# Grouped attention: the two halves of the last three heads' partitions change places by transfers within SBUF, one sine product in place of two

## The reference, cut to what matters

```python
q = _layernorm(q, q_norm_w, q_norm_b)
k = _layernorm(k, k_norm_w, k_norm_b)
...
def _rope(x, cos, sin):
    xr, xi = (x[..., 0::2], x[..., 1::2])
    c, s = (cos[None, None], sin[None, None])
    out = jnp.stack([xr * c - xi * s, xr * s + xi * c], axis=-1)
    return out.reshape(x.shape)
q = _rope(q, cos, sin)
k = _rope(k, cos, sin)
k = jnp.repeat(k, rep, axis=1)
v = jnp.repeat(v, rep, axis=1)
scores = jnp.einsum('bhqd,bhkd->bhqk', q, k) / math.sqrt(D)
scores = jnp.where(causal[None, None], scores, -jnp.inf)
attn = jax.nn.softmax(scores, axis=-1)
out = jnp.einsum('bhqk,bhkd->bhqd', attn, v)
out = out.transpose(0, 2, 1, 3).reshape(B, S, H * D)
out = out * jax.nn.sigmoid(gate)
return out @ w_o.T
```

## Time and profile before

| | us |
|---|---|
| median of 3 runs | 1878.19 (1874.29 to 1879.25) |
| the profiled execution | 1874.4 |
| its span, first to last instruction | 1873.1 |
| PE busy | 1588.7 (85%) |
| DVE busy | 1240.9 (66%) |
| ACT busy | 910.1 (49%) |
| POOL busy | 334.2 (18%) |

### The profile page before, as it was taken

How to read it: one execution, slowest core, us unless ns; L and a number is a source line. 1 busy time by engine, 2 the same in 40 slices (tenths; PEclk the granted TensorE clock), 3 DMA queues, 4 the chain that set the end, 5 groups by cost and what they waited for, 6 DMA issues and landing times. The chain is left out here.

```text
span 1873.1 us, 16334 instructions
## 1 busy us (share of the span) xinstructions
PE 1588.7 (85%) x5242; PEld 861.0 (46%) x5242; DVE 1240.9 (66%) x2009; ACT 910.1 (49%) x1615; POOL 334.2 (18%) x208
## 2 busy tenths in 40 slices
PE   5998788788899999977989989767778777799998
PEld 2564354367544434433444444323323332347776
DVE  7685574433356446567786877569679899856665
ACT  5454344443322212268787878534565543325443
POOL 1001231231001101100000000000038666313332
PEclk8998899886789999988999989776789999999999
DMA  2003762350030000011010000200200000011110
GB/s 76 1 1 99 274 223 99 75 101 1 6 131 0 0 15 0 12 61 40 1 47 1 17 18 1 78 18 1 74 0 1 0 1 1 18 39 48 56 49 23
DMA packets 40729, 79.81 MB, mean 43 GB/s; under 512 B 9058, under 2 KB 26420, under 8 KB 38342
## 3 DMA queue, kind: packets, MB, share of 16 engines
q1 hardware_dynamic: 35558, 53.08, 9.4%
q0 software_dynamic: 5088, 25.69, 3.9%
HBM read 70.49 MB, written 7.22 MB: 41 GB/s over the span
## 5 line engine op out<-in xcount | busy, mean ns | idle before, releaser
L2872 POOL TENSOR_TENSOR s_bu<-s_rep,s_du 128x1024 f32<-128x1024 f32 x64 | 150.6, 2354 | 682.4 <-ACT s_rep L2789 599.3
L2726 DVE TENSOR_TENSOR_SCAN s_bu<-bank,s_bu 128x1024 f32<-128x1024 f32 x64 | 146.0, 2282 | 13.6 <-ACT bank L2798 13.5
L2961 PE MATMUL bank<-s_bu,ident 128*128 128x512 f32 x256 | 132.3, 642 | 0.9 <-DVE s_dl L2673 0.2
L159 PE MATMUL bank<-e_xs,e_wsp 128*128 128x512 f32 x528 | 127.7, 391 | 0.7 <-issue 0.7
L2798 ACT ACTIVATE bank<-s_dl,s_an 128x510 f32<-128x510 f32 x128 | 82.8, 682 | 75.4 <-DVE s_bu L2726 75.3
L159 PEld LDWEIGHTS bank<-e_xs,e_wsp 128*128 128x128 f32 x528 | 99.1, 188 | 22.7 <-issue 1.9
L159 PE MATMUL bank<-r_am,r_b 128*128 128x512 f32 x240 | 106.0, 593 | 1.4 <-DVE r_am L1712 1.4
L159 PE MATMUL bank<-conditioned,g_wqk 128*128 128x512 f32 x160 | 84.2, 654 | 0.3 <-POOLq L147 0.3
L1770 ACT ACTIVATE r_sl<-bank 128x512 f32<-128x512 f32 x28 | 16.7, 597 | 136.4 <-PE bank L159 133.2
L3067 DVE TENSOR_TENSOR e_s<-e_s,bank 128x512 f32<-128x512 f32 (+1 forms) x50 | 34.3, 687 | 69.3 <-ACT e_s L3199 69.3
L2742 DVE TENSOR_TENSOR s_bu<-s_bu,bank 128x1024 f32<-128x1024 f32 x64 | 76.6, 1197 | 5.1 <-PE bank L2892 4.9
(11 more groups left out here) (500 smaller groups left out, 3662.4 us busy)
## 6 DMA issues: line engine op xcount, KB each, us to landing
e_wgu<-in_e_gu SPq DMA_DIRECT2D x22, 256.0 KB, 2.6
b_vw<-b_values SPq DMA_DIRECT2D x48, 64.0 KB, 3.5
e_wd<-in_e_down SPq DMA_DIRECT2D x22, 128.0 KB, 2.6
r_w<-in_r_w SPq DMA_DIRECT2D x3, 896.0 KB, 8.4
g_wqk<-in_g_qk SPq DMA_DIRECT2D x4, 640.0 KB, 6.1
g_wgv<-in_g_gv SPq DMA_DIRECT2D x4, 640.0 KB, 3.9
g_wo<-in_g_wo SPq DMA_DIRECT2D x4, 512.0 KB, 3.5
m_sorted<-m_zero SPq DMA_DIRECT2D x1, 1920.0 KB, 13.2
```

What stands on the lines that cost most here:

```text
L159: last = e.matmul(out, lhs, rhs, start=start and n == 0, stop=stop and n == len(pairs) - 1, skip_group_check=True)
L2726: e.tensor_tensor_scan(b, flat(k.pairs[n % 2][:, :, :]), b, 0.0, ALU.mult, ALU.add).then_inc(k["s_scanned"].up(), 1)
L2872: e.tensor_tensor(m.bu[n % m.NBU][:, :, :], m.rep[:, 2 * np:2 * np + 2, :], m.du[:, et, half(h)].unsqueeze(1).to_broadcast([P, 2, HALF]), ...
L2961: summed = e.matmul(banks[6][:, :], k.ident[:, :], m.bu[(n - 1) % m.NBU][:, i, :], start=np == 0 and i == 0, stop=np == m.NP - 1 and i == ...
```

## The change

For the query heads j = 2, 3 and 4 the two halves of the partitions of the scaled vector are copied crosswise into the `turn` buffer by two transfers of 64 partitions x 512 f32 (128 KB each), issued by SP. DVE then needs one sine product over all 128 partitions, in place on `turn`, where it had two of 64 partitions. Its order is now cosine product, wait for the transfers, sine product, and a difference in place of the sum, since the sign of the sine table now falls on the other half. For j = 0 and j = 1 the four instructions stay as they were. In SP's queue the 24 pairs of transfers are put between the loads, and the loads of `wo`, `wgv` and of the next stage's weights come behind the pairs of the unit before them.

```diff
+def grouped_swap_sync(k, e, f, j):
+    m, n = k.grouped, 5 * f + j
+    e.wait_ge(*k["g_affine"].at(n + 1))
+    e.wait_ge(*k["g_roped"].at(n - 1))
+    for a, b in ((slice(0, 64), slice(64, P)), (slice(64, P), slice(0, 64))):
+        e.dma_start(m.turn[n % 2][a, :], m.rs[b, j, :]).then_inc(k[f"g_swapped{j}"].up(16), 16)
...
     for g in range(m.KV):
         if g:
+            for j in range(2, 5):
+                grouped_swap_sync(k, e, 2 * g - 2, j)
             if g > 1:
                 e.wait_ge(*k["g_projected"].at(10 * (g - 1)))
             e.dma_start(m.wqk[g % 2][:, :, :], d["g_qk"][g]).then_inc(k[f"load_g_qk{g % 2}"].up(16), 16)
+            for j in range(2, 5):
+                grouped_swap_sync(k, e, 2 * g - 1, j)
...
+    for j in range(2, 5):
+        grouped_swap_sync(k, e, m.STEPS - 2, j)
     e.wait_ge(*k["q_scales"].at(1))
...
+    for j in range(2, 5):
+        grouped_swap_sync(k, e, m.STEPS - 1, j)
     e.wait_ge(*k["g_down"].at(4 * m.KV - 4))
...
     e.wait_ge(*k["g_affine"].at(n + 1))
-    e.tensor_tensor(both(turn[0:64, :]), both(r[64:P, :]), table(m.rsn[64:P, :]), ALU.mult).then_inc(k.v_steps.sem, 1)
-    e.tensor_tensor(both(turn[64:P, :]), both(r[0:64, :]), table(m.rsn[0:64, :]), ALU.mult).then_inc(k.v_steps.sem, 1)
-    e.tensor_tensor(both(o), both(r), table(m.rc[:, :]), ALU.mult).then_inc(k.v_steps.sem, 1)
...
+    if j < 2:
...
+    else:
+        e.tensor_tensor(both(o), both(r), table(m.rc[:, :]), ALU.mult).then_inc(k.v_steps.sem, 1)
+        k.v_tick()
+        e.wait_ge(*k[f"g_swapped{j}"].at(32 * (f + 1)))
+        e.tensor_tensor(both(turn[:, :]), both(turn[:, :]), table(m.rsn[:, :]), ALU.mult).then_inc(k.v_steps.sem, 1)
     e.wait_ge(k.v_steps.sem, k.v_tick())
-    e.tensor_tensor(o, o, turn[:, :], ALU.add).then_inc(k["g_roped"].up(), 1)
+    e.tensor_tensor(o, o, turn[:, :], ALU.add if j < 2 else ALU.subtract).then_inc(k["g_roped"].up(), 1)
```

More of the change, by code:

```diff
@@ L1998, in grouped_rope @@
     e.wait_ge(*k["g_affine"].at(n + 1))
-    e.tensor_tensor(both(turn[0:64, :]), both(r[64:P, :]), table(m.rsn[64:P, :]), ALU.mult).then_inc(k.v_steps.sem, 1)
-    e.tensor_tensor(both(turn[64:P, :]), both(r[0:64, :]), table(m.rsn[0:64, :]), ALU.mult).then_inc(k.v_steps.sem, 1)
-    e.tensor_tensor(both(o), both(r), table(m.rc[:, :]), ALU.mult).then_inc(k.v_steps.sem, 1)
-    k.v_tick()
-    k.v_tick()
+    if j < 2:
+        e.tensor_tensor(both(turn[0:64, :]), both(r[64:P, :]), table(m.rsn[64:P, :]), ALU.mult).then_inc(k.v_steps.sem, 1)
+        e.tensor_tensor(both(turn[64:P, :]), both(r[0:64, :]), table(m.rsn[0:64, :]), ALU.mult).then_inc(k.v_steps.sem, 1)
+        k.v_tick()
+        k.v_tick()
+        e.tensor_tensor(both(o), both(r), table(m.rc[:, :]), ALU.mult).then_inc(k.v_steps.sem, 1)
+    else:
+        e.tensor_tensor(both(o), both(r), table(m.rc[:, :]), ALU.mult).then_inc(k.v_steps.sem, 1)
+        k.v_tick()
+        e.wait_ge(*k[f"g_swapped{j}"].at(32 * (f + 1)))
+        e.tensor_tensor(both(turn[:, :]), both(turn[:, :]), table(m.rsn[:, :]), ALU.mult).then_inc(k.v_steps.sem, 1)
     e.wait_ge(k.v_steps.sem, k.v_tick())
-    e.tensor_tensor(o, o, turn[:, :], ALU.add).then_inc(k["g_roped"].up(), 1)
+    e.tensor_tensor(o, o, turn[:, :], ALU.add if j < 2 else ALU.subtract).then_inc(k["g_roped"].up(), 1)
 def grouped_greatest(k, e, a, u):
```

## The result

| | before | changed kernel |
|---|---|---|
| median of 20 runs each, in turn on one chip, us | 1877.02 (1866.76 to 1881.22) | 1866.1 (1860.83 to 1876.11) |
| ratio to before, 95% interval | | 0.9941 (0.9926 to 0.9956) |
| the profiled execution, us | 1874.4 | 1872.89 |
| its span, us | 1873.1 | 1871.4 |

The change makes the kernel 0.59% faster, 11 us. The profiled execution of the changed kernel gained only 1.5 us on the one before, so this answer comes from the timed runs. What the trace can tell is the stage, the stretch of the grouped attention. From the issue of the cosine table's load to the issue of the next stage's `q_sb` load it took 453.91 us before (793.07 to 1246.98) and 442.47 now (798.72 to 1241.19): 11.44 us less, close to what the ratio says. The rest of the span took 1419.2 us in the one execution and 1428.9 in the other, with the same instructions.

A forecast was written before the change was run, and what follows sets the result against it. No engine was taken as saturated; DVE's time counts where PE's order runs through it, at ropes 2 and 4. 5.2 + 4.9 = 10.1 us off 1874.4 gives 1864.3, named 1868 us for the median; range 1859 to 1879.

The forecast's parts named there:

- the two places: Ropes 2 and 4, where PE's order runs through DVE: 5.2 + 4.9 = 10.1 us less.
- One of its own signs of being wrong: Stretches at 1.2 GHz on PE longer or shorter in sum by more than 5 us would mean the clock made the difference.
- L: Time from the end of ACT's affine step to the landing of both transfers, 2.4 to 2.7 us.
- Rope 2: DVE at the start of a pass: no wait, 0.71 us saved in 7 passes, 0.27 in pass 2; sum 5.2.
- Rope 3: DVE waits 0.6 us for the transfers; nothing gained, lateness up to some 0.8 us covered, costed at nothing.
- Rope 4: PE's weight load for head 3's scores gains 0.61 us in each of 8 passes, 4.9 us.
- The clock: TensorE at 1.2 GHz in stretches behind idle time: change too small to remove them; chance 0.05 for each side.
- The loads: Gate and value weights, behind the third pair in SP's queue, start near 986.6, land at 990.5, covered by 15 us.
- (a): Transfers land late, L between 3.1 and 4.2: rope 2 saves little or loses; 1873 to 1882 us; chance 0.22.
- (b): Slower: the wait at rope 2 becomes the chain from L = 4.35 on; 1919 us at L = 6.3; chance 0.08.
- (c): All 24 DVE products count, in ropes 2, 3 and 4: 17.0 us less, 1861 us; chance 0.10.
- (d): TensorE's 1.2 GHz stretches change in 2 or 3 of 8 passes: 1858 or 1878 us; chance 0.05 for each side.

The follow-up runs named there:

- the fill: Matmuls that nobody reads, added where PE would stand idle at the start of a pass; ratio to before 0.9979 added to before, 0.9916 added to the changed kernel.
- rope 4 alone: Exchange by transfers for rope 4 only, ropes 2 and 3 as in before; ratio to before 0.9941, stage 440.46 us.
- the second profile of before: The kernel before, unchanged, profiled once more; stage 452.42 us against 453.91 in the first profile.
- the filled kernel of before: The kernel before with unread matmuls added where PE would stand idle; ratio to before 0.9979, stage 449.54 us.
- each part alone: Exchange by transfers for rope 4 only, and in another kernel for rope 2 only; ratios to before 0.9941 and 0.9954.

## Why the prediction came out right, step by step

The time was right, 1868 forecast and 1866.1 measured, and so was the mechanism at the ropes: two of three places count, rope 3 is hidden. But the sum of 10.1 us is right partly by luck, because two errors cancel: the two places give about 7.4 us, since rope 4 was taken too high, and some 4 us more came that the prediction had set at nothing. One of its own signs of being wrong came true, too: the stretches at 1.2 GHz are 23 us shorter in sum, where it had named 5.

**L.** Forecast 2.4 to 2.7, measured 2.8 to the landing and 2.9 to DVE's start. The issue took 0.50 us where a load's 0.37 was taken, the landing 2.3 where the cosine table's 2.0 was. That table is a single load, and the trace of before had more rows of 128 KB, which the prediction didn't use: 22 loads of `e_wd` at 2.6 us, 15 transfers to `m_results` at 1.9, and single ones up to 5.1. The time that the transfers have was off too. The cosine product starts 2.03 us behind the affine step and lets the next one start 0.6 us later, so it is 2.6 us and not 2.84. The estimate by the Trainium skill (DMA: Bandwidth & Descriptors, Anatomy of one DMA and Rules for kernel authors) was 3.0 with a wait of 0.16 us at rope 2; measured were 2.9 and 0.23. The measurement agrees with the page: the landing that it gives for 128 KB, 2.3 us, is the one measured, although that section of the page is on transfers that GpSimd issues and these were issued by SP. The two issues stand 0.50 us apart and each lands in 2.3, so no run here shows by itself that the halves serialize. Nor did any run move both halves by one transfer, or issue them from two engines.

```profile
e_wd<-in_e_down SPq DMA_DIRECT2D x22, 128.0 KB, 2.6
...
m_results<-m_o SPq DMA_DIRECT2D x15, 128.0 KB, 1.9
```

**Rope 2**, forecast 0.71 a pass, gave 0.63 (11.97 to 11.34). The wait of 0.23 did not come off the 0.71: without transfers rope 2 ended 0.95 us sooner than before, since the products also start sooner behind each other (last section), and the wait took 0.32 of that back. Forecast 5.2 us; with the 0.51 and 0.32 of passes 1 and 2 it is 4.6. In pass 2 the prediction allowed 0.27, because DVE's maximum then waits for PE's scores; rope 2 itself gained 0.32 there, because its wait is longer. What the pass gained by it can't be told from the clock's share.

**Rope 3**, forecast nothing, with a wait of 0.6 us. The wait is 1.23 and rope 3 ends 0.3 us later behind rope 2 than before (22.98 to 22.67 in pass 3, where rope 2 gained 0.63). It is hidden: slowing its transfers by one more microsecond cost 0.47 us in odd passes and nothing in pass 6. Of 1.0 us some 0.5 were still covered, which with the 0.3 used up already is the 0.8 us of cover that the prediction read.

**Rope 4** is the mis-sized term: forecast 0.61 us a pass from the idle time at the weight load (0.85 - 0.24), 4.9 us in all, measured 0.28 in less disturbed passes and 0.35 with the fill, 8 x 0.28 = 2.2 or 2.8 us. The idle time did vanish as forecast. But a weight load runs ahead of the matmuls: while it waited, PE itself didn't stand still. Ahead of head 3's scores in before, pass 4:

```profile
995.46 1.02 PE L159 MATMUL bank<-g_sq,ones 128*128 128x512 f32 x2
996.50 0.49 PE L2284 MATMUL bank<-g_q 128*128 128x128 f32 x2
```

The matmuls ahead end at 996.48. From their start to the scores it was 1.04 us, and it is 0.86 with rope 4 alone. From head 2's scores to head 3's PE took 4.71 us in pass 4 of the second profile of before and 4.53 with rope 4 alone, 0.18 less; by the next scores the difference is 0.27 (with the fill 0.27 and 0.35). Where that second part comes from was not found. In pass 8, where PE does stand still, the product is worth 0.96.

**The clock** was set at nothing with a chance of 0.05 to each side. By the less disturbed passes the two places give 0.92 us a pass, 8 x 0.92 = 7.4 us of the stage's 11.44, if all eight passes are taken alike. The other 4 lie where the stretches at 1.2 GHz differ. Pass 1 gained 2.45 us and the tail 3.76, pass 6 lost 0.08 against the path's 0.9. That the clock can do this is shown twice: by the same kernel's pass 4 at 46.42 and 48.50, and by the two tails with the fill. That it gave 4 us on the average of the timed runs is only argued, from one or two traces of each kernel, and the timed runs speak rather against it: with the fill, which holds the clock in passes 3 to 7, the changed kernel still gains 0.63% on the filled kernel of before, no less than the 0.59% without. In the tail the fill leaves 24 us at 1.2 GHz in before and 17 in the changed kernel, and from the one to the other the tail gets 4.2 us shorter (73.61 to 69.39), more than the ropes of pass 8 give. So the clock's share of the 11 us stays open. What stays open too is why each part alone, 0.9941 and 0.9954, gives nearly as much as both. Their traces show 65 and 82 us at the lower level, against 102 and 99 in the two profiles of before, but what places a stretch was not found.

**The loads** were covered as forecast, by 12.7 us instead of 15. They went out 18.8 us after the start of the pass, as forecast (986.6 is 18.8 behind 967.82); the landing took 0.9 us longer, and the value projection came 1.3 us sooner in the shorter pass.

**The rivals.** (a) missed by 0.2 us of L; cutting rope 2's transfers raised L to 3.9 there and the gain was nil, about as its price said (between 1873 at 3.55 and 1882 at 4.2). (b) has the right mechanism at the wrong L. (c), all 24 products, is out: rope 3's and rope 1's savings went into waits for transfers, and with no transfers at all an odd pass gains 1.24 us, not 2.1. (d) was given too little weight: not one stretch gone in 2 or 3 passes, but several shorter or better placed, though the 4 us that they may have given are less than its price of 10.

## What to carry to other kernels

Before a product is traded for a transfer, compare the time that the transfer has (from its input to its first use) with issue, landing and start together: with 2.6 us for a transfer of 2.9 the saving was 0.63 us a pass, at rope 3, where the wait was 1.23 us, it was nothing, and a microsecond more at rope 2 turned the whole gain to zero. The idle time of a weight load was an upper bound for what PE gained there, 0.61 us read and 0.28 measured; look whether the matmuls ahead end where the next ones start. Where the clock wanders between its levels, compare single passes with the same stretches, or fill the idle time, before two edits are said to add up or not.

## What was not expected of the hardware

A product of 64 partitions that reads the other half of the partitions started later behind its predecessor than one of 128 that stays in its own. Behind the inverse (start to start) it took 993.40 to 993.60 before, 0.20 us, and 994.70 to 994.78 now, 0.08. From the start of the inverse to the end of rope 4 it was 3.05 us and is 2.08: 0.97 saved by taking out a product of 0.71. No run separates the crossing from the number of partitions.

A transfer of 64 partitions of 2 KB within SBUF took SP 0.46 to 0.93 us to issue (median 0.50) and landed in 2.2 to 2.7 us.

Idle matmuls made the kernel a little faster: with 1.00 granted in passes 3 to 7, before went to 0.9979 (0.9964 to 0.9993), with 16 matmul instructions more in each of those passes (148 against 132, 179 against 163).
